# A one-core early-fusion block: the tiles of its expert phase taken in pairs, the down product two pairs behind the gate product

## The chip, the cores and the metric

The kernel runs on one core of one Trainium2 chip. The metric is the device time of one execution in microseconds (us). A core has a matrix engine (PE, with its weight loads, PEld), a vector engine (DVE), an activation engine (ACT), GpSimd (POOL) and a queue engine (SP) that only issues DMAs. Each engine runs its own list of instructions in order; between engines, semaphores are counted up by the one and waited for by the other.

## What is computed

64 images are cut into 36 patches and projected; with a class token and 77 text rows each gives 114 tokens of 256 values, so there are 64 x 114 = 7296 tokens. Then a linear-attention block and a mixture of eight experts follow, each behind a layernorm and with a residual. The change is in the experts:

```python
def _L0_ffn_ref(hidden_states, gate_w, w_gate, w_up, w_down):
    x = hidden_states.reshape(-1, h)
    logits = x @ gate_w.T
    top_v = jnp.max(logits, axis=-1)
    sel = jnp.argmax(logits, axis=-1)
    rw = jax.nn.sigmoid(top_v)
    out = jnp.zeros_like(x)
    for e in range(8):
        mask = (sel == e).astype(x.dtype)
        xs = x * (rw * mask)[:, None]
        g = xs @ w_gate[e].T
        u = xs @ w_up[e].T
        out = out + u * jax.nn.silu(g) @ w_down[e].T
    return out.reshape(b, s, h)
...
h = h + _L0_attn_ref(_layernorm(h, axis=-1), ...)
h = h + _L0_ffn_ref(_layernorm(h, axis=-1), ...)
```

## The kernel before

**Main loop.** 32 pairs of images run through tokeniser, layernorm, attention and routing, to about 345 us. POOL writes every token's row (256 values, and its layernorm's shift and gain and its number) to its place in a list in HBM that is sorted by expert (L652, an indirect DMA for each image, x64). Of 64 tiles of 128 sorted rows, SP loads the first 32 while the loop still runs and the rest once the last image is scattered. The places of the later tiles are worked out in `late_count`, `late_slots` and `late_rows`, which stand in the lists of PE and DVE between the first steps of the expert phase, and so do the routing's last two `tanh` on ACT.

**Expert phase.** Tile t goes through these hands, all in `tile_step(j)`, which each engine runs for j up to 66:

- ACT: xs(t), the layernorm's scale and shift of the rows (L908), four steps ahead.
- PE: turn_x(t), two transposes of xs into PSUM (L1620), two steps ahead; ACT and DVE split them into a high and a low part, xsT_hi (L898) and xsT_lo (L933).
- PE: gate(t), the gate and up products, 2 x 3 matmuls of 256 columns into b_kg (L1351 to L1353).
- ACT: silu of the gate half (L894). DVE: act_u, its product with the up half (L1263).
- PE: turn_a(t), one transpose of act_u (L1629) in step t+1; ACT and DVE split it into actT_hi (L904) and actT_lo (L933).
- PE: down(t), 3 matmuls of 256 columns (L1351 to L1353 into b_w or b_att) in step t+2. DVE: result(t), down plus the row itself, for the residual (L1279), step t+2.
- POOL: an indirect store of result(t) to the output, 131 KB (L716), step t+2.

PE's step j is gate(j), turn_x(j+2), turn_a(j-1), down(j-2). ACT's is silu(j), xsT_hi(j+2), actT_hi(j-1), xs(j+4). DVE's is act_u(j), xsT_lo(j+2), actT_lo(j-1), result(j-2). The order is that of the code, and nothing else chooses it. The expert of a tile is a number in a register of PE, from which the address of its weights is formed before each product (`expert(t)`, L1593; 16 such registers are reloaded in `load_experts`).

Rings: xs and xsT hold four tiles, silu_g, act_u and actT two, result four. turn_x alternates between PSUM banks b_v and b_t, the gate product between the two banks of b_kg. turn_a and down share b_w until tile `SOLO` = 24 and then alternate between b_w and b_att. DVE writes result(t) only when the store of tile t-4 has landed (semaphores stored0 to stored3), and PE writes turn_a and down into a bank only when DVE has read what stood in it.

Of the kernel before, what the change touches and what calls it, by code (L numbers as in the profile page):

```python
# [24 lines left out]
P = 128  # L25
# [46 lines left out]
SOLO = 24  # L72
# [37 lines left out]
def build(nc, x, txt, w_tok, pos, wq, bq, wkgv, wo, wo_rows, bias, bv, bo_col, wgu, wdown, ids, consts, slots, out):  # L110
    scratch = nc.dram_tensor("sorted_rows", (EXPERTS * REGION + P, ROW), F32, kind="Internal").ap()

    with ExitStack() as ctx:
# [83 lines left out]
        with ExitStack() as room:  # L197
# [33 lines left out]
            silu_g = sb("silu_g", [P, 2, INNER], at=room)  # L231
            act_u = sb("act_u", [P, 2, INNER], at=room)
            actT_hi, actT_lo = parts("actT", [P, 2, P], room)
# [25 lines left out]
        def turn_a_bank(t):  # L259

            return (b_w if t.n < SOLO or t.n % 2 == 0 else b_att)[:, 0, 0:P]

        def down_bank(t):

            return (b_w if t.n < SOLO or t.n % 2 == 0 else b_att)[:, 1, 0:D]

# [27 lines left out]
        def b_tile(banks, t, width, start=0):  # L294
            return banks[t.slot(2)][:, start:start + width]
# [102 lines left out]
        DRAIN_B, STEPS_B = 5, range(5, TILES + 3)  # L398
# [185 lines left out]
        def _(pool):  # L584
# [126 lines left out]
            def tile_step(j):  # L711
                if (j - 2).within(TILES):
                    t = j - 2
                    k = t.slot(4)
                    pool.wait_ge(result_ready, t.upto())
                    G.indirect_dma_start(  # L716
                        out=out, out_offset=bass.IndirectOffsetOnAxis(ap=rows_all[:, t.n, ID:ID + 1].bitcast(I32), axis=0),
                        in_=result[:, k, :], in_offset=None,
                        bounds_check=TOKENS - 1, oob_is_err=False).then_inc(stored[k], 16)

            straight(range(0, DRAIN_B), tile_step)
            straight(STEPS_B, tile_step)


        @block.scalar
        def _(act):
# [163 lines left out]
            def tile_step(j):  # L890
                if j.within(TILES):
                    t = j
                    act.wait_ge(gu_done, t.upto())
                    S.activation(silu_g[:, t.slot(2)], b_tile(b_gu, t, INNER), ACT.Silu).then_inc(silu_ready, 1)  # L894
                if (j + 2).within(TILES):
                    t = j + 2
                    act.wait_ge(turn_x_done, t.upto())
                    S.copy(xsT_hi[:, t.slot(4)], b_tile(b_x, t, KC * P).rearrange("p (k t) -> p k t", k=KC)).then_inc(xsT_hi_ready, 1)  # L898
                if (j - 1).within(TILES):
                    t = j - 1  # L900
                    act.wait_ge(turn_a_done, t.upto())
                    if t.had(2):
                        act.wait_ge(down_done, t.upto(2))
                    S.copy(actT_hi[:, t.slot(2)], turn_a_bank(t)).then_inc(actT_hi_ready, 1)  # L904
                if (j + 4).within(TILES):
                    t = j + 4
                    act.wait_ge(row_loaded[t.slot(4)], 16 * t.rounds(4))
                    S.activation(xs[:, t.slot(4)], rows_all[:, t.n, 0:D], ACT.Identity,  # L908
                                 bias=rows_all[:, t.n, SHIFT:SHIFT + 1], scale=rows_all[:, t.n, GAIN:GAIN + 1]).then_inc(xs_ready, 1)
# [14 lines left out]
            straight(STEPS_B, tile_step)  # L924


        @block.vector
        def _(dve):
            V = nc.vector
# [866 lines left out]
```

## Time and profile before

| what | us |
|---|---|
| median of 3 runs (lowest, highest) | 494.29 (491.44, 494.54) |
| the profiled execution | 494.96 |
| its span, first to last instruction | 493.2 |
| mean granted clock of PE, share of full speed | 0.976 |
| main loop, its last work | about 345 |
| expert phase: gate product of tile 0 starts | 359.95 |
| gate product of tile 8 starts | 378.88 |
| gate product of tile 62 starts | 476.37 |
| last instruction ends | 493.17 |

Busy over the whole span: PE 450.4 us (91%), DVE 384.6 (78%), POOL 301.9 (61%), ACT 268.7 (54%). These shares are mostly the main loop's. A row of a timeline gives an instruction's start in us, its length, engine, line, operation, the buffers (out<-in), and in square brackets the idle time of the engine just before it with what ended it; "issue" is time for which the profile shows no wait that ended last. For a group, a number behind x is a count, then come busy time and the mean ns of one. Ends of matmuls are modelled by the profile; their starts are recorded.

### The profile page before, as it was taken

The numbers are of one execution on the slowest core, as the hardware profiler recorded it, in microseconds if no ns is written. First come the engines' busy times: TensorE is split into PE (matmuls) and PEld (weight loads), VectorE is DVE, ScalarE is ACT, GpSimd is POOL, SyncE is SP. The second block draws the span as 40 slices with busy tenths as digits, with TensorE's granted clock in tenths as the row PEclk, the third lists the DMA queues.
The fourth block names the chain that finished last, engine by engine and source line by source line (L and its number), as shares of the span: only waits on it lengthen the run. The fifth ranks groups of instructions, "written<-read, shape, count | busy, mean of one in ns | idle before, by whom it ended". The sixth has DMA issues, their size and how long they took to land. (4 is left out here: it accounts for less than half of the span.)

```text
span 493.2 us, 12451 instructions
## 1 busy us (share of the span) xinstructions
PE 450.4 (91%) x3728; PEld 437.6 (89%) x3728; DVE 384.6 (78%) x1272; ACT 268.7 (54%) x706; POOL 301.9 (61%) x694
## 2 busy tenths in 40 slices
PE   4999999999999999999999999999768989888781
PEld 4999999999999999999999999998757879787770
DVE  5758679999999899989999988977566767676661
ACT  5444455455566566566456356544345667666650
POOL 6405215777777777777777767765565546455453
PEclk9999999999999999999999999999788999999995
DMA  8862122324231321111111211176235762111120
GB/s 290 301 202 83 58 57 69 114 70 119 72 105 32 88 77 33 56 44 35 52 46 35 55 45 44 44 192 165 62 112 161 218 194 76 65 67 62 61 69 13
DMA packets 35007, 46.14 MB, mean 94 GB/s; under 512 B 8937, under 2 KB 27100, under 8 KB 34944
## 3 DMA queue, kind: packets, MB, share of 16 engines
q1 hardware_dynamic: 25722, 30.23, 20.9%
q0 software_dynamic: 9216, 15.12, 10.1%
q8 instruction: 32, 0.52, 0.5%
q14 instruction: 31, 0.25, 0.2%
q10 hardware_dynamic: 6, 0.01, 0.0%
HBM read 26.61 MB, written 17.17 MB: 89 GB/s over the span
## 5 line engine op out<-in xcount | busy, mean ns | idle before, releaser
L716 POOL DMA_INDIRECT out<-result,rows_all x64 | 62.7, 980 | 51.9 <-issue 26.2
L652 POOL DMA_INDIRECT sorted_rows<-rows,place x64 | 78.0, 1218 | 20.3 <-issue 9.7
L800 ACT ACTIVATE den<-b_att,z_eps 114x32 f32<-114x32 f32 x32 | 9.2, 288 | 77.2 <-PE b_att L1465 74.0
L817 ACT ACTIVATE q_exp<-b_w,bq_s 128x228 f32<-128x228 f32 x64 | 28.9, 452 | 29.7 <-PE b_w L1353 29.7
L1263 DVE TENSOR_TENSOR act_u<-b_kg,silu_g 128x128 f32<-128x128 f32 x64 | 18.5, 289 | 30.4 <-ACT silu_g L894 21.2
L1351 PE MATMUL b_kg<-wkgv_hi,xnT_hi 128*114 128x264 f32 x128 | 41.9, 328 | 0.0
L1351 PE MATMUL b_w<-wo_hi,attnT_hi 128*114 128x264 f32 x124 | 41.0, 331 | 0.0
L908 ACT ACTIVATE xs<-rows_all 128x256 f32<-128x256 f32 x64 | 39.4, 617 | 0.0
L1351 PE MATMUL b_kg<-wgu_hi,xsT_hi 128*128 x128 | 37.4, 292 | 1.8 <-issue 1.8
L1351 PE MATMUL b_w<-xnT_hi,wq_hi 128*128 128x256 f32 x128 | 38.6, 301 | 0.4 <-DVE logits L1068 0.3
L894 ACT ACTIVATE silu_g<-b_kg 128x128 f32<-128x128 f32 x64 | 17.8, 278 | 38.7 <-PE b_kg L1353 34.3
L1351 PE MATMUL b_v<-wkgv_hi,xnT_hi 128*114 128x256 f32 x128 | 38.8, 303 | 0.0
L1401 PE MATMUL b_att<-v_sb,k_sb 114*128 114x136 f32 x256 | 37.4, 289 | 0.0
L1465 PE MATMUL b_att<-kv_sb,qT 128*114 128x136 f32 x256 | 35.6, 283 | 1.9 <-DVE qT L1035 1.9
L1353 PE MATMUL b_kg<-wgu_hi,xsT_lo 128*128 x128 | 36.8, 287 | 0.0
L1352 PE MATMUL b_kg<-wgu_lo,xsT_hi 128*128 x128 | 36.6, 286 | 0.0
L1352 PE MATMUL b_kg<-wkgv_lo,xnT_hi 128*114 128x264 f32 x128 | 36.5, 285 | 0.0
L1353 PE MATMUL b_kg<-wkgv_hi,xnT_lo 128*114 128x264 f32 x128 | 36.3, 283 | 0.0
L1352 PE MATMUL b_w<-xnT_lo,wq_hi 128*128 128x256 f32 x128 | 36.1, 282 | 0.0
L1353 PE MATMUL b_w<-xnT_hi,wq_lo 128*128 128x256 f32 x128 | 35.9, 281 | 0.0
L1353 PE MATMUL b_v<-wkgv_hi,xnT_lo 128*114 128x256 f32 x128 | 35.9, 280 | 0.0
L1352 PE MATMUL b_v<-wkgv_lo,xnT_hi 128*114 128x256 f32 x128 | 35.8, 280 | 0.0
(244 smaller groups left out, 1793.8 us busy)
## 6 DMA issues: line engine op xcount, KB each, us to landing
rows_all<-sorted_rows SPq DMA_DIRECT2D x64, 130.0 KB
rows_all<-in_x SPq DMA_DIRECT2D x18, 384.0 KB, 4.7
rows_all<-in_txt SPq DMA_DIRECT2D x32, 154.0 KB
rows_all<-in_wgu SPq DMA_DIRECT2D x8, 256.0 KB, 3.0
rows_all<-patch_out SPq DMA_DIRECT2D x48, 36.0 KB
sorted_rows<-tail_rows SPq DMA_DIRECT2D x9, 130.0 KB
rows_all<-in_wdown SPq DMA_DIRECT2D x8, 128.0 KB, 3.5
sorted_rows<-rows,place POOLq DMA_INDIRECT x64
```

Source lines behind the costliest of these rows:

```text
L652: G.indirect_dma_start(out=scratch[0:EXPERTS * REGION, :], out_offset=bass.IndirectOffsetOnAxis(ap=place[:, k, b:b + 1], axis=0), in_=rows ...
L716: G.indirect_dma_start(out=out, out_offset=bass.IndirectOffsetOnAxis(ap=rows_all[:, t.n, ID:ID + 1].bitcast(I32), axis=0), in_=result[:, k ...
L800: S.activation(den[:].rearrange("p b (k h) -> p b k h", k=KC), heads[:, :, :, P:KVW], ACT.Identity, bias=z_eps[0:TOK, :]).then_inc(den_don ...
L817: S.activation(q_exp[:, c, :], at, ACT.Exp, bias=bq_s[:, c:c + 1])
L894: S.activation(silu_g[:, t.slot(2)], b_tile(b_gu, t, INNER), ACT.Silu).then_inc(silu_ready, 1)
L908: S.activation(xs[:, t.slot(4)], rows_all[:, t.n, 0:D], ACT.Identity, bias=rows_all[:, t.n, SHIFT:SHIFT + 1], scale=rows_all[:, t.n, GAIN: ...
L1263: V.tensor_tensor(act_u[:, t.slot(2)], b_tile(b_gu, t, INNER, INNER), silu_g[:, t.slot(2)], ALU.mult).then_inc(act_ready, 1)
L1351: T.matmul(to, left_hi, right_hi, start=start, stop=False)
L1352: T.matmul(to, left_hi, right_lo, start=False, stop=False)
L1353: return T.matmul(to, left_lo, right_hi, start=False, stop=stop)
L1401: last = T.matmul(b_att[:, b, c * KVW:(c + 1) * KVW], k_sb[:, b, c * P:(c + 1) * P], v_sb[:, b, c, :], start=True, stop=True)
L1465: last = T.matmul(b_att[0:TOK, b, c * KVW:(c + 1) * KVW], qT[:, c, b * TOK:(b + 1) * TOK], kv_sb[:, b, c, :], start=True, stop=True)
```

## The change

Each engine now runs `duo_step(j)` for a pair of tiles (m = tiles 2m and 2m+1), 32 pairs.

- ACT and DVE take both tiles of a pair in one instruction: silu, act_u, xsT_hi, xsT_lo, actT_hi, actT_lo and result, each twice as wide. xs stays an instruction for each tile. For that silu_g, act_u and actT hold four tiles instead of two, and a gate bank, a turn_x bank, a turn_a half and a down half hold both tiles of a pair.
- PE runs the same matmuls for each tile and waits and signals once for a pair. Its step is gate(j), turn_a(j-1), turn_x(j+2), down(j-2), all of pairs. So turn_a now stands before turn_x, and down(j) is two pair-steps behind gate(j).
- DVE's step begins with result(j-3) and then has act_u(j), actT_lo(j-1), xsT_lo(j+2). ACT's is silu(j), actT_hi(j-1), xsT_hi(j+2), then two xs(j+3).
- The result ring still has four tiles, so two pairs: one result instruction waits for both stores of the pair two before it. POOL waits once and then issues both stores.
- The first `tanh`, `late_slots` and `late_rows` stand between pair-steps, where they stood between tile-steps. `SOLO` = 12 pairs is the same tile as before.

The diff's core (the sizes of the rings and what only renames is left out):

```diff
...
-            def tile_step(j):
-                if (j - 2).within(TILES):
-                    t = j - 2
-                    k = t.slot(4)
-                    pool.wait_ge(result_ready, t.upto())
...
+            def duo_step(j):
+                if (j - 3).within(DUOS):
+                    m = j - 3
+                    pool.wait_ge(result_ready, m.upto())
+                    for t in tiles_of(m):
+                        k = t.slot(4)
+                        G.indirect_dma_start(
...
             attention_high(PAIRS - 2)
             S.activation(silu_ahead[:], bq_s[:, 0:1], ACT.Silu)
-            tile_step(Turn(0, -4))
-            tile_step(Turn(0, -3))
+            duo_step(Turn(0, -3))
             tanh(PAIRS - 4)
             denominators(PAIRS - 1)
             tanh(PAIRS - 3)
             attention_high(PAIRS - 1)
-            straight(range(-2, 1), tile_step)
+            straight(range(-2, 1), duo_step)
             tanh(PAIRS - 2)
-            tile_step(Turn(0, 1))
+            duo_step(Turn(0, 1))
             tanh(PAIRS - 1)
-            straight(range(2, DRAIN_B), tile_step)
-            straight(STEPS_B, tile_step)
+            straight(STEPS_B, duo_step)
...
+            def duo_step(j):
+                if (j - 3).within(DUOS):
+                    m = j - 3
+                    dve.wait_ge(down_done, m.upto())
+                    if m.had(2):
+                        for t in tiles_of(m):
+                            dve.wait_ge(stored[t.slot(4)], 16 * t.rounds(4, 4))
+                    V.tensor_tensor(duo(result, m), down_bank(m).rearrange("p (t d) -> p t d", t=DUO),
+                                    rows_all[:, DUO * m.n:DUO * m.n + DUO, 0:D], ALU.add).then_inc(result_ready, 1)
...
-            straight(range(0, 2), tile_step)
+            duo_step(Turn(0, 0))
             late_slots()
-            straight(range(2, 4), tile_step)
+            duo_step(Turn(0, 1))
             late_rows()
-            straight(range(4, 7), tile_step)
-            straight(range(7, TILES + 3), tile_step)
+            straight(STEPS_B, duo_step)
...
+                    pe.wait_ge(xsT_lo_ready, m.upto())
+                    for t in tiles_of(m):
+                        e, to = expert(t), b_gu[m.slot(2)][:, t.slot(2) * D:t.slot(2) * D + 2 * INNER]
+                        for k in range(KC):
+                            last = product(to, (xsT_hi[:, t.slot(4), k, :], xsT_lo[:, t.slot(4), k, :]),
+                                           (wgu_hi[:, bass.ds(e, 1), k, :], wgu_lo[:, bass.ds(e, 1), k, :]), k == 0, k == KC - 1)
                     last.then_inc(gu_done, 1)
...
+                if (j - 1).within(DUOS):
+                    m = j - 1
+                    pe.wait_ge(act_ready, m.upto())
...
+                    for t in tiles_of(m):
+                        last = T.transpose(turn_a_bank(m)[:, t.slot(2) * P:(t.slot(2) + 1) * P], act_u[:, t.slot(4)], ident)
+                    last.then_inc(turn_a_done, 1)
...
+                if (j - 2).within(DUOS):
+                    m = j - 2
+                    pe.wait_ge(actT_lo_ready, m.upto())
...
+                    for t in tiles_of(m):
+                        e = expert(t)
+                        last = product(down_bank(m)[:, t.slot(2) * D:(t.slot(2) + 1) * D], (actT_hi[:, t.slot(4)], actT_lo[:, t.slot(4)]),
+                                       (wdown_hi[:, bass.ds(e, 1), :], wdown_lo[:, bass.ds(e, 1), :]), True, True)
+                    last.then_inc(down_done, 1)
...
```

PE's list in the middle of the expert phase. Before, from turn_x (L1620) over turn_a (L1629) and down into the next gate product; ISA and REGISTER_ALU are the register work on the expert's number:

```order
3177 L1620 MATMUL b_t<-con_s,xs 128x128 [waits xs_ready]
3178 L1620 MATMUL b_t<-con_s,xs 128x128
3179 L1629 MATMUL b_w<-con_s,act_u 128x128 [waits actT_lo_ready,act_ready]
3180 L1351 ISA [waits result_ready,actT_lo_ready]
3181 L1351 MATMUL b_att<-wdown_hi,actT_hi 128x256
3182 L1352 REGISTER_ALU
3183 L1352 MATMUL b_att<-wdown_lo,actT_hi 128x256
3184 L1353 MATMUL b_att<-wdown_hi,actT_lo 128x256
3185 L1351 ISA [waits xsT_lo_ready]
3186 L1351 MATMUL b_kg<-wgu_hi,xsT_hi 128x256
3187 L1352 REGISTER_ALU
3188 L1352 MATMUL b_kg<-wgu_lo,xsT_hi 128x256
```

After, the same place of a pair, from turn_a (now L1630) over turn_x (L1642) and the down products of both tiles:

```order
2741 L1630 MATMUL b_w<-con_s,act_u 128x128 [waits actT_lo_ready,act_ready]
2742 L1630 MATMUL b_w<-con_s,act_u 128x128
2743 L1642 MATMUL b_v<-con_s,xs 128x128 [waits xs_ready]
2744 L1642 MATMUL b_v<-con_s,xs 128x128 x3
2745 L1602 ISA [waits result_ready,actT_lo_ready]
2746 L1360 MATMUL b_w<-wdown_hi,actT_hi 128x256
2747 L1361 REGISTER_ALU
2748 L1361 MATMUL b_w<-wdown_lo,actT_hi 128x256
2749 L1362 MATMUL b_w<-wdown_hi,actT_lo 128x256
2750 L1602 ISA
2751 L1360 MATMUL b_w<-wdown_hi,actT_hi 128x256
2752 L1361 REGISTER_ALU
```

turn_a moved ahead of turn_x and comes in twos; the down product's first tile alone waits; each tile keeps its three matmuls and its register work.

DVE's list there, before, from a result on: L933 is the low part, first of xs, then of the activation:

```order
1148 L1279 TENSOR_TENSOR result<-b_att,rows_all 128x256 [waits stored3,down_done]
1149 L1263 TENSOR_TENSOR act_u<-b_kg,silu_g 128x128 [waits silu_ready]
1150 L933 TENSOR_TENSOR xsT_lo<-b_v,xsT_hi 128x256 [waits xsT_hi_ready]
1151 L933 TENSOR_TENSOR actT_lo<-b_att,actT_hi 128x128 [waits actT_hi_ready]
1152 L1279 TENSOR_TENSOR result<-b_w,rows_all 128x256 [waits stored0,down_done]
1153 L1263 TENSOR_TENSOR act_u<-b_kg,silu_g 128x128 [waits silu_ready]
1154 L933 TENSOR_TENSOR xsT_lo<-b_t,xsT_hi 128x256 [waits xsT_hi_ready]
1155 L933 TENSOR_TENSOR actT_lo<-b_w,actT_hi 128x128 [waits actT_hi_ready]
1156 L1279 TENSOR_TENSOR result<-b_att,rows_all 128x256 [waits stored1,down_done]
```

After, a whole pair-step and the next result (L1275, was L1279):

```order
1104 L1275 TENSOR_TENSOR result<-b_w,rows_all 128x512 [waits stored1,stored0,down_done]
1105 L1280 TENSOR_TENSOR act_u<-b_kg,silu_g 128x256 [waits silu_ready]
1106 L942 TENSOR_TENSOR actT_lo<-b_w,actT_hi 128x256 [waits actT_hi_ready]
1107 L942 TENSOR_TENSOR xsT_lo<-b_t,xsT_hi 128x512 [waits xsT_hi_ready]
1108 L1275 TENSOR_TENSOR result<-b_att,rows_all 128x512 [waits stored3,stored2,down_done]
```

Eight instructions for two tiles became four, result moved to the head of the step, actT_lo moved ahead of xsT_lo, and a result waits for two stores.

ACT's list at the first tiles, before, from silu of tile 0: L765 is the routing's `tanh`:

```order
457 L894 ACTIVATE silu_g<-b_kg 128x128 [waits gu_done]
458 L898 CAST xsT_hi<-b_v 128x256 [waits turn_x_done]
459 L908 ACTIVATE xs<-rows_all 128x256 [waits row_loaded0]
460 L765 ACTIVATE tanh_top<-top_n 114x2 [waits field_step,top_n_ready]
461 L894 ACTIVATE silu_g<-b_kg 128x128 [waits gu_done]
462 L898 CAST xsT_hi<-b_t 128x256 [waits turn_x_done]
463 L904 CAST actT_hi<-b_w 128x128 [waits turn_a_done]
464 L908 ACTIVATE xs<-rows_all 128x256 [waits row_loaded1]
465 L765 ACTIVATE tanh_top<-top_n 114x2 [waits field_step,top_n_ready]
```

After, from silu of pair 0:

```order
459 L902 ACTIVATE silu_g<-b_kg 128x256 [waits gu_done]
460 L913 CAST xsT_hi<-b_v 128x512 [waits turn_x_done]
461 L918 ACTIVATE xs<-rows_all 128x256 [waits row_loaded2]
462 L918 ACTIVATE xs<-rows_all 128x256 [waits row_loaded3]
463 L773 ACTIVATE tanh_top<-top_n 114x2 [waits field_step,top_n_ready]
464 L902 ACTIVATE silu_g<-b_kg 128x256 [waits gu_done]
465 L909 CAST actT_hi<-b_w 128x256 [waits turn_a_done]
466 L913 CAST xsT_hi<-b_t 128x512 [waits turn_x_done]
467 L918 ACTIVATE xs<-rows_all 128x256 [waits row_loaded0]
468 L918 ACTIVATE xs<-rows_all 128x256 [waits row_loaded1]
469 L773 ACTIVATE tanh_top<-top_n 114x2 [waits field_step,top_n_ready]
```

Each `tanh_top` stands behind the work of a pair instead of a tile, and actT_hi moved ahead of xsT_hi.

## Rows read from the trace of the kernel before

**Rows 1.** Windows: length; PE, PEld, DVE, ACT, POOL busy (count); PEclk, DMA share, GB/s.

```profile
359.95:378.88 18.93, 14.91 (x94) 13.73 (x95) 11.56 (x44) 9.38 (x32) 13.22 (x30) 0.82 0.44 132
378.88:476.37 97.49, 84.81 (x650) 76.81 (x649) 66.63 (x217) 65.59 (x216) 52.61 (x54) 1.00 0.34 107
476.37:493.17 16.80, 4.60 (x29) 3.40 (x27) 4.02 (x13) 1.45 (x7) 6.13 (x7) 0.70 0.10 33
```

**Rows 2.** Timeline, PE, one unstalled tile step: start, length, line, operation.

```profile
430.55 0.38 PE L1620 MATMUL b_v<-con_s,xs 128*128 128x128 f32 x2
430.76 0.27 PE L1629 MATMUL b_att<-con_s,act_u 128*128 128x128 f32 x1
...
431.22 0.28 PE L1351 MATMUL b_kg<-wgu_hi,xsT_hi 128*128 x1
...
431.93 0.38 PE L1620 MATMUL b_t<-con_s,xs 128*128 128x128 f32 x2
```

**Rows 3.** Groups by shape, ACT: out<-in, shapes, count, busy us, mean ns.

```profile
L894 ACT ACTIVATE silu_g<-b_kg 128x128 f32<-128x128 f32 x64 | 17.8, 278 | 38.7 <-PE b_kg L1353 34.3 <-issue 3.8 <-remote 0.4
L898 ACT CAST xsT_hi<-b_v 128x256 fp32r<-128x256 f32 x32 | 12.0, 375 | 2.2 <-PE b_v L1620 1.4 <-PE b_t L1620 0.4
...
L791 ACT COPY v_sb<-b_v 114x512 f32<-114x512 f32 x18 | 10.6, 587 | 11.7 <-PE b_v L1353 10.8 <-issue 0.9
```

**Rows 4.** Groups by shape, DVE, columns as above.

```profile
L1060 DVE TENSOR_TENSOR rows<-b_w,rows_all 114x512 f32<-114x512 f32 x31 | 21.4, 692 | 9.5 <-PE b_w L1353 7.8 <-issue 1.7
...
L1263 DVE TENSOR_TENSOR act_u<-b_kg,silu_g 128x128 f32<-128x128 f32 x64 | 18.5, 289 | 30.4 <-ACT silu_g L894 21.2 <-issue 9.0
L1279 DVE TENSOR_TENSOR result<-b_w,rows_all 128x256 f32<-128x256 f32 x44 | 18.4, 419 | 3.2 <-PE b_w L1353 1.4 <-remote 1.3
```

**Rows 5.** Timeline, all engines, around a late signal (tile 48).

```profile
450.60 0.98 POOL L716 DMA_INDIRECT out<-result,rows_all  x1 [0.30 <-issue]
450.66 0.28 PE L1353 MATMUL b_kg<-wgu_hi,xsT_lo 128*128 x1
...
452.07 0.98 POOL L716 DMA_INDIRECT out<-result,rows_all  x1 [0.49 <-issue]
...
452.18 0.38 PE L1620 MATMUL b_t<-con_s,xs 128*128 128x128 f32 x2
...
453.00 0.28 ACT L894 ACTIVATE silu_g<-b_kg 128x128 f32<-128x128 f32 x1 [2.15 <-PE b_kg L1353]
...
453.66 0.33 PE L1629 MATMUL b_w<-con_s,act_u 128*128 128x128 f32 x1 [1.10 <-issue]
...
454.24 0.41 DVE L1279 TENSOR_TENSOR result<-b_w,rows_all 128x256 f32<-128x256 f32 x1
...
455.45 0.98 POOL L716 DMA_INDIRECT out<-result,rows_all  x1 [2.41 <-DVE result L1279]
```

**Rows 6.** Waits, 378 to 478 us: waiter, releaser, total us, times, longest.

```profile
ACT silu_g L894 <- PE b_kg L1353: 25.1, 33, 2.2
```

**Rows 7.** Timeline, POOL and DVE: stores of tiles 58 and 59, result of 63.

```profile
476.92 0.98 POOL L716 DMA_INDIRECT out<-result,rows_all  x1 [0.30 <-issue]
...
478.41 0.98 POOL L716 DMA_INDIRECT out<-result,rows_all  x1 [0.51 <-issue]
...
482.59 0.42 DVE L1279 TENSOR_TENSOR result<-b_att,rows_all 128x256 f32<-128x256 f32 x1 [0.39 <-PE b_att L1353]
```

**Rows 8.** Busy time by stretch after the store at 476.92; DMA share, GB/s last.

```profile
478.25:479.00 0.75, 0.36 (x4) 0.16 (x2) 0.00 (x0) 0.00 (x0) 0.59 (x1) 1.00 0.50 175
```

**Rows 9.** Timeline, ACT, PE and POOL where the first tiles meet the last pair.

```profile
362.62 0.19 ACT L765 ACTIVATE tanh_top<-top_n 114x2 f32<-114x2 f32 x1
...
367.60 0.20 ACT L765 ACTIVATE tanh_top<-top_n 114x2 f32<-114x2 f32 x1 [3.01 <-POOL top_n L627]
...
369.04 0.30 PE L1629 MATMUL b_w<-con_s,act_u 128*128 128x128 f32 x1 [2.57 <-DVE actT_lo L933]
...
371.81 1.01 POOL L716 DMA_INDIRECT out<-result,rows_all  x1 [0.30 <-issue]
```

More of the change, by code:

```diff
@@ L230, in build @@
             xsT_hi, xsT_lo = parts("xsT", [P, 4, KC, P], room)
-            silu_g = sb("silu_g", [P, 2, INNER], at=room)
-            act_u = sb("act_u", [P, 2, INNER], at=room)
-            actT_hi, actT_lo = parts("actT", [P, 2, P], room)
+            silu_g = sb("silu_g", [P, 4, INNER], at=room)
+            act_u = sb("act_u", [P, 4, INNER], at=room)
+            actT_hi, actT_lo = parts("actT", [P, 4, P], room)
             result = sb("result", [P, 4, D], at=room)
@@ L292, in build, with duo, tiles_of @@
         tile_ends = b_att[0:1, 1, EARLY_AT + 32:EARLY_AT + 32 + ENDS_W]
-        def b_tile(banks, t, width, start=0):
-            return banks[t.slot(2)][:, start:start + width]
+        def duo(ring, m):
+            first = m.slot(2) * DUO
+            return ring[:, first:first + DUO]
+        def tiles_of(m):
+            return [Turn(0, DUO * m.n + k) for k in range(DUO)]
         s_const = sem("s_const")
@@ L888, in _ @@
                 step(i)
[L890 to L909, printed above, removed]
@@ new lines, in duo_step @@
+            def duo_step(j):
+                if (j - 3).within(DUOS):
+                    m = j - 3
+                    dve.wait_ge(down_done, m.upto())
+                    if m.had(2):
+                        for t in tiles_of(m):
+                            dve.wait_ge(stored[t.slot(4)], 16 * t.rounds(4, 4))
+                    V.tensor_tensor(duo(result, m), down_bank(m).rearrange("p (t d) -> p t d", t=DUO),
+                                    rows_all[:, DUO * m.n:DUO * m.n + DUO, 0:D], ALU.add).then_inc(result_ready, 1)
+                if j.within(DUOS):
+                    m = j
+                    dve.wait_ge(silu_ready, m.upto())
+                    V.tensor_tensor(duo(act_u, m), b_gu[m.slot(2)].rearrange("p (t w) -> p t w", t=DUO)[:, :, INNER:], duo(silu_g, m),
+                                    ALU.mult).then_inc(act_ready, 1)
+                if (j - 1).within(DUOS):
+                    m = j - 1
+                    dve.wait_ge(actT_hi_ready, m.upto())
+                    low(duo(actT_lo, m), turn_a_bank(m).rearrange("p (t n) -> p t n", t=DUO), duo(actT_hi, m)).then_inc(actT_lo_ready, 1)
+                if (j + 2).within(DUOS):
+                    m = j + 2
+                    dve.wait_ge(xsT_hi_ready, m.upto())
+                    low(duo(xsT_lo, m).rearrange("p t k n -> p (t k n)"), b_x[m.slot(2)],
+                        duo(xsT_hi, m).rearrange("p t k n -> p (t k n)")).then_inc(xsT_lo_ready, 1)
@@ new lines, in duo_step @@
+                if (j + 2).within(DUOS):
+                    m = j + 2
+                    if m.n == 0:
+                        pe.wait_ge(v_ready, PAIRS)
+                    if m.n == 1:
+                        pe.wait_ge(attnT_lo_ready, PAIRS - 1)
+                    pe.wait_ge(xs_ready, m.upto())
+                    for t in tiles_of(m):
+                        for k in range(KC):
+                            at = (t.slot(2) * KC + k) * P
+                            last = T.transpose(b_x[m.slot(2)][:, at:at + P], xs[:, t.slot(4), k * P:(k + 1) * P], ident)
+                    last.then_inc(turn_x_done, 1)
```

125 lines of the change are left out of this document (50 added, 75 removed).

## The prediction

> **What bounds the kernel now.** I read the page's slices first: PE is full up to about 345 us and the change leaves those instructions alone. Then I cut the expert phase into stretches by the starts of its gate products [rows 1]. The middle one, tiles 8 to 62, is 54 tiles in 97.49 us, 1.81 us a tile, at a granted clock of 1.00. No engine is full in it: PE 84.81, DVE 66.63, ACT 65.59, POOL 52.61. So the phase is bound by waiting between engines, and the question is what is waited for.
>
> The timeline of PE gives the step without a stall [rows 2]: from one turn_x (430.55) to the next (431.93) is 1.38 us, of it turn_x 0.21, turn_a and down 0.46, gate 0.71. 54 x 1.38 = 74.5, so 97.49 - 74.5 = 23.0 us are lost in this stretch, 0.43 a tile. The others have room in a 1.38 step: DVE 66.63 / 54 = 1.23, ACT 1.21. Their instructions are short, 0.28 to 0.42 us, and wider ones cost little more [rows 3, 4].
>
> The timeline around tile 48 shows how the loss arises [rows 5]. PE's last matmul of gate(48) starts at 450.66 and ends, by the model, at 450.94. silu, which waits for it alone, starts at 453.00, 2.06 us later. silu and act_u follow at once, and turn_a starts at 453.66, 0.66 after silu's start. PE had finished its turn_x at 452.56 and stood for 1.10. So gate's signal came late, not ACT. In this order PE has turn_x 0.21, turn_a and down 0.46, the next gate 0.71 and turn_x 0.21 between the end of gate(t) and turn_a(t), 1.59 us. The chain needs 0.66, so a signal may be late by 0.93 for nothing, and 2.06 - 0.93 = 1.13 is the stall seen. The waits view says how often: ACT's silu waited 25.1 us for PE in 33 waits, the longest 2.2 [rows 6]. What makes the signal late the trace doesn't say. Two facts stand near it: silu started (453.00) just as the second of two POOL stores ended (452.07 + 0.98 = 453.05), and PE's register work on the expert's number exists in this phase.
>
> A rule bears on this. In the Trainium skill, "Perfetto Trace Analysis", section "Tensor Engine Instruction (MATMUL, LD_WEIGHTS)", a matmul's reported end is an estimate, and its semaphore goes out only when PSUM has acknowledged the writes. By that rule the 2.06 need not be a delay between engines: PE itself may be behind its records, which is the third rival below.
>
> **The change part by part, per pair of tiles.**
>
> PE: the same matmuls and register instructions, so 2 x 1.38 = 2.76 us without a stall. Fewer waits are worth nothing where the step has no stall.
>
> ACT: silu two of 0.278 become one of 0.375, -0.18; actT_hi likewise -0.18; xsT_hi two of 0.375 become one of 0.587 (the nearest row of that width) -0.16 [rows 3]. 2 x 1.21 = 2.43 becomes 1.91. DVE: act_u two of 0.289 become 0.419, -0.16; actT_lo the same; xsT_lo and result two of 0.419 become 0.692, -0.15 each [rows 4]. 2.47 becomes 1.85. Both hide under PE's 2.76 before and after; the direct gain is nothing. POOL: two stores of 0.98 with 0.30 between, 2 x 1.28 = 2.56 [rows 5], still under 2.76, but its cover is only 0.20.
>
> The order is what counts. After, between the end of gate(j) and turn_a(j) PE has turn_a(j-1), turn_x(j+2), down(j-2) and gate(j+1), the whole 2.76. The chain grows by the wider silu and act_u, 0.66 + 0.10 + 0.13 = 0.89. So the room is 1.87 where it was 0.93. The stall of tile 48 would shrink from 1.13 to 0.19, and there is one gate signal for two tiles. Queued behind turn_a on PE stand turn_x(j+2) and down(j-2); down(j-2) has a step more than it needs.
>
> Bounds of the step: nothing lost, 1.38 a tile; all the loss stays, 1.81. By tile 48 alone nearly everything is won; against that, turn_x, turn_a and down send signals too, whose lateness I can't read, and a pair's results arrive at DVE and POOL in lumps. I take the middle, 1.60. Gain in the middle stretch: 54 x (1.81 - 1.60) = 11.3 us.
>
> The result ring. It holds two pairs, so result(m) waits for both stores of m-2. The loop is result 0.69 [rows 4], result's end to the store's start 0.80 (454.65 to 455.45 [rows 5]), stores 0.98 + 0.30 + 0.98, and landing L: 3.75 + L against two steps, 5.52 at 1.38 a tile, 6.40 at 1.60. L from below: the store that ended at 476.92 + 0.98 = 477.90 [rows 7] still moved data at 175 GB/s from 478.25 to 479.00 [rows 8], 0.75 x 175 = 131 KB, its whole size, so L is at least 1.10. From above: result(63), which needs the store of tile 59 (478.41 + 0.98 = 479.39), stood at 482.59 [rows 7], so L is at most 3.20. The loop is 4.85 to 6.95. Since the data ended at 1.10, I take L near 1.1 to 1.6, and the ring costs nothing.
>
> The Trainium skill, "DMA: Bandwidth & Descriptors", section "Anatomy of one DMA — SWDGE (gpsimd) path", gives such a DMA about 2.0 us fixed, most of it the write's receipt, beside its bytes. An estimate with that behind the second issue, 3.75 + 2.0 + 0.30 = 6.05, is 1.51 us a tile: by it the relief would stop at about 478 us, and by the rows it needn't. No row here times the receipt.
>
> Start. The last two tanh were issued at 362.62 and 367.60, the second after 3.01 of waiting for POOL; PE stood 2.57 before 369.04, and the first store left at 371.81 [rows 9]. After, the second tanh stands behind a pair's work more, so it and what POOL does after it come later by a tile or two (1.4 to 2.8 us); but when it is done, PE and ACT are about two tiles further. Net 0, bounds -3 and +3. Drain: the last pair passes turn_a, down, result and two stores; fewer instructions, wider ones, one step more. -0.3, bounds -0.5 and +0.7.
>
> Sum: 494.96 (the profiled execution: span 493.2 and 1.8 around it) - 11.3 + 0 - 0.3 = 483.4. The median of the runs is 0.7 below the profiled one, so 483.
>
> **The rivals.** (1) Near-full relief: T = 1.38 to 1.50, 494.96 - 54 x 0.43 - 0.3 = 471 to 494.96 - 16.7 - 0.3 = 478. For it: tile 48's own arithmetic. Against: other signals, and POOL's 2.56 of 2.76 leaves no slack for a lump. (2) The ring binds: L near its upper bound, 6.95 / 4 = 1.74 a tile, 494.96 - 3.8 - 0.3 = 491; with L at 2.9, 1.66 and 487. For it: result(63) came so late. Against: 131 KB had moved by 1.10. (3) The change doesn't do what it says: the late signals are PE's own pace with these instructions, a register operation and three or six matmuls a tile, all unchanged. Then T stays 1.78 to 1.85 and the time 493 to 497. For it: the profile's ends are modelled and PE issues the same list; against: PE's unstalled steps of 1.38 hold the same register work. (4) Slower: the stores now leave in streaks. If a store holds back signals (453.00 against 453.05 [rows 5]), a streak holds one for 0.98 + 0.30 + 0.98 and the 0.61 from the store's end (453.05) to turn_a (453.66), 2.87; less the room of 1.87 that is 1.0 a pair, T = 1.88, 494.96 + 3.8 - 0.3 = 498.5, and with the start's bound up to 502. It decides where a pair's gate signal is later than 1.87 + 0.86 = 2.73 us on the mean (0.86 is what two tiles lose now). Against: the longest wait seen is 2.2 [rows 6], although stores already followed each other at 0.30 and 0.49 there.
>
> **How the numbers follow.** Partial relief (1.50 to 1.68, 478 to 488) 0.42; near-full relief 0.18; the ring 0.10; unchanged pace 0.20; slower 0.10. A measurement of this kernel tells about 1% from nothing: 489.4 and 499.2 are the marks. Faster: 0.42 + 0.18 + 0.07 of the ring's = 0.67. Same: 0.20 + 0.03 = 0.23. Slower: 0.10. The range 472 to 495 leaves out the slower case, about 0.05 of the unchanged pace above 495 and 0.02 below 472, 0.17 in all.
>
> **What would show it.** In the changed kernel's windows, gate to gate over the pairs 4 to 31 (54 tiles) should take about 86 us (1.60 a tile), with PE's 84.8 busy nearly filling it; 75 means full relief, 96 or more none. PE's waits for act_u before turn_a should be few and short; silu's waits for PE may stay late. DVE's result should not be released by a store; if it is, the ring binds. silu should be one instruction near 0.375, act_u near 0.42. The second tanh should start near 369 to 370. Wrong it would be above all if PE's step of a pair never comes near 2.76: then the loss was PE's own.

## The result, and the profile after

The kernel after took 495.68 us (median of 20 runs, 493.02 to 499.18) beside 493.78 for the kernel before (20 runs): a ratio of 1.0036, interval 1.0019 to 1.0054. The forecast was 483. The change moved the time by less than 1%, and upwards. The profiled execution took 496.18 us, its span 494.4, at a mean granted clock of 0.966.

The stretches of the kernel after by its gate products: start to pair 4 (tile 8), pair 4 to pair 31 (tile 62), and the rest. Columns as in [rows 1].

```profile
358.60:371.79 13.19, 12.20 (x87) 11.23 (x88) 9.37 (x33) 7.68 (x20) 9.25 (x25) 0.88 0.34 105
371.79:471.87 100.08, 84.93 (x646) 80.28 (x645) 55.79 (x107) 57.71 (x132) 53.24 (x55) 0.93 0.36 110
471.87:494.40 22.53, 6.17 (x36) 5.15 (x34) 4.39 (x9) 1.13 (x3) 9.82 (x11) 0.71 0.14 45
```

The middle takes 100.08 us where it took 97.49, 1.85 a tile. Its gate products come 7.1 us earlier at pair 4 and 4.5 earlier at pair 31, because gate products now run further ahead of the results. So the results compare better: that of pair 4 starts at 386.85 and that of pair 31 at 483.63, 96.8 us, where tiles 9 and 63 stood at 386.71 and 482.59, 95.9 us. The rate of finished tiles is what it was, 1.79 us against 1.78.

DVE and ACT did get lighter: DVE is busy 55.79 us instead of 66.63, ACT 57.71 instead of 65.59. The groups by shape between 378 and 478 us, columns as in [rows 3]:

```profile
L1280 DVE TENSOR_TENSOR act_u<-b_kg,silu_g 128x256 f32<-128x256 f32 x27 | 11.4, 424 | 24.8 <-ACT silu_g L902 15.8 <-issue 8.8
L902 ACT ACTIVATE silu_g<-b_kg 128x256 f32<-128x256 f32 x27 | 10.4, 383 | 30.4 <-PE b_kg L1362 23.8 <-remote 5.9 <-issue 0.5
```

PE is at a granted clock of 0.93 in the middle, where it was at 1.00. In slices of 20 us (the last of 17) the clock column, third from the right, reads 0.86, 0.97, 0.91, 1.00 and 0.90:

```profile
378.00:398.00 20.00, 16.01 (x107) 14.55 (x107) 10.49 (x21) 11.04 (x26) 8.83 (x9) 0.86 0.77 222
...
418.00:438.00 20.00, 16.98 (x130) 16.28 (x129) 11.14 (x23) 12.11 (x29) 10.53 (x11) 0.91 0.20 69
```

Missing clock is 2.8 + 0.6 + 1.8 + 0 + 1.7 = 6.9 us of full speed. It is counted over PE's waits too, so that is the most it can have cost; the kernel before reads 1.00 in all five slices. The parts at the lower level (1.2 GHz) come behind waits of PE: from 427 to 433 us, around its wait of 2.10 at 428.29 (below), the granted clock is 0.76.

Where PE stood, the waits view of PE says, 372 to 484 us (waiter, releaser, total us, times, longest):

```profile
PE b_t L1642 <- ACT xs L918: 7.4, 6, 2.0
PE b_att L1630 <- DVE act_u L1280: 2.1, 1, 2.1
PE b_att L1630 <- issue: 1.9, 1, 1.9
PE b_w L1630 <- issue: 1.8, 2, 1.2
PE b_v L1642 <- ACT xs L918: 1.6, 2, 0.8
```

turn_x waiting for ACT's xs is new; the kernel before has no such wait in its middle. Within the middle stretch alone PE waited 4.5 us before turn_a (L1630) and 9.6 before turn_x (L1642), whatever ended the wait.

The timeline around the latest signal shows the mechanism (PE's rows between left out but for the last matmuls of a gate product):

```profile
422.62 0.69 DVE L1275 TENSOR_TENSOR result<-b_w,rows_all 128x512 f32<-128x512 f32 x1 [0.32 <-DMA out<-result,rows_all]
422.66 0.98 POOL L725 DMA_INDIRECT out<-result,rows_all  x1 [0.30 <-issue]
...
422.79 0.28 PE L1362 MATMUL b_kg<-wgu_hi,xsT_lo 128*128 x1
...
424.10 0.98 POOL L725 DMA_INDIRECT out<-result,rows_all  x1 [0.46 <-issue]
...
425.39 0.98 POOL L725 DMA_INDIRECT out<-result,rows_all  x1 [0.30 <-issue]
...
425.92 0.28 PE L1362 MATMUL b_kg<-wgu_hi,xsT_lo 128*128 x1
427.39 0.38 ACT L902 ACTIVATE silu_g<-b_kg 128x256 f32<-128x256 f32 x1 [4.83 <-PE b_kg L1362]
...
428.29 0.44 PE L1630 MATMUL b_att<-con_s,act_u 128*128 128x128 f32 x2 [2.10 <-DVE act_u L1280]
```

The gate product ends at 423.07 and its silu starts at 427.39, 4.32 us late, 1.02 after the last of a row of POOL stores ended (426.37). Meanwhile PE went through turn_a, turn_x, down and a whole further gate product. In the trace's semaphore records PE's signals for this gate, turn_a, turn_x, down and the next gate stand at 427.37, 427.41, 427.47, 427.55 and 427.67, and the one before them at 422.30. PE did 3 us of work after the gate whose signals then came out within 0.30 us. So they were held back, not late because PE was slow. Only PE's were: of the signals from 372 to 482 us that can be matched to their instruction, 50 of PE's 102 stand over 0.1 us behind its end, while those of ACT (80) and DVE (86) all stand 0.01 behind. Some records are missing for each engine.

### The profile page after: what moved, and what is told of

Same layout as the page of the kernel before. It is cut to its first block, busy times and chain, and to the rows that moved or that the text cites. A ratio compares the mean times of both kernels' runs of the same rounds, so it can differ in the third digit from the quotient of the medians.

```text
span 494.4 us, 11973 instructions
## 1 busy us (share of the span) xinstructions
PE 449.1 (91%) x3728; PEld 440.0 (89%) x3728; DVE 373.0 (75%) x1144; ACT 260.1 (53%) x610; POOL 300.9 (61%) x694
## 4 chain that ended last, share of the span: by engine, by line
PE 82%; ACT 4%; issue 4%; DVE 3%; another core or an unknown queue 2%; POOL 2%; DMA 1%; POOLq 0%; SPq 0%; DVEq 0%
PE b_w L1360 7%; PE b_kg L1362 7%; PE b_w L1361 7%; PE b_w L1362 7%; PE b_kg L1360 7%; PE b_att L1410 7%; PE b_kg L1361 6%; PE b_att L1474 6%; PE b_v L1360 3%; PE b_v L1362 3%; PE b_v L1361 3%; PE b_t L1488 2%; PE b_t L1423 2%; ACT xs L918 2%
## 5 line engine op out<-in xcount | busy, mean ns | idle before, releaser
L1360 PE MATMUL b_kg<-wgu_hi,xsT_hi 128*128 x128 | 38.4, 300 | 0.2
L1361 PE MATMUL b_kg<-wgu_lo,xsT_hi 128*128 x128 | 37.6, 293 | 0.0
L1280 DVE TENSOR_TENSOR act_u<-b_kg,silu_g 128x256 f32<-128x256 f32 x32 | 13.6, 424 | 29.4 <-ACT silu_g L902 18.5
L1361 PE MATMUL b_w<-wo_lo,attnT_hi 128*114 128x264 f32 x124 | 35.7, 288 | 0.0
L1362 PE MATMUL b_w<-wo_hi,attnT_lo 128*114 128x264 f32 x124 | 35.6, 287 | 0.0
```

Of the source, the lines that this page charges most:

```text
L1280: V.tensor_tensor(duo(act_u, m), b_gu[m.slot(2)].rearrange("p (t w) -> p t w", t=DUO)[:, :, INNER:], duo(silu_g, m), ALU.mult).then_inc(ac ...
L1360: T.matmul(to, left_hi, right_hi, start=start, stop=False)
L1361: T.matmul(to, left_hi, right_lo, start=False, stop=False)
L1362: return T.matmul(to, left_lo, right_hi, start=False, stop=stop)
```

## The experiments

**What the chips do.** The groups of runs met two kinds of conditions. In one the kernel before takes 493 to 495 us (the comparison above and the runs c, d and g; "late chips" below), in the other 475.0 to 475.6 (e and f; "prompt chips"). The record numbers the chips 15 (c), 1 (d) and 14 (g), and 1 (e) and 3 (f). The number 1 stands on both sides, 26 minutes apart, and the record doesn't say whether it is the same chip. So "late" and "prompt" name what a group met, and not a property of the chip that was shown. Within one group the kernel before was timed between the others and stayed on its side. The main loop takes the same time on both (in the kernel after the first silu starts at 360.7 to 361.6 on late chips and at 362.6 on a prompt one). Each run stands beside the kernel before of its own group, and a theory's letter holds within its group. I measure lateness as silu's start minus the modelled end of its gate product, mean over all silu (good to about 0.02 us). It also counts time in which ACT was still busy. The signal records tell the two apart: in d3, d4 and all e and f runs every gate signal stands 0.01 us behind its gate's end, so what lateness these have (0.08 to 0.15) is ACT's own queue in the first pairs.

**e1 and e2: no register work.** In the kernels after and before:

```diff
-                return pe.snap(expert_of[...][...], min_val=0, max_val=EXPERTS - 1)
+                return t.n // 8
```

> The kernel after, but the expert of tile t is the constant t//8 instead of a number read from a table into PE registers: the same matmuls, no register work on PE (the output is that of other experts, since each tile meets fixed weights). In the kernel after the results of pairs 4 to 31 span 386.85 to 483.63, 96.8 us for 54 tiles, 1.79 a tile, as before. Theory A (PE's late signals come from the register work): with it gone the same stretch falls to 75 to 82 us and the time to about 475 to 482. Theory B (the streaks of POOL stores hold PE's signals back): no change, 94 to 98 us and 494 to 497. Theory C (the ring of two pairs of results binds): no change either.

> The kernel before with the same edit: constant experts, no register work on PE (the output is that of other experts). Theory A: the 0.43 us a tile lost goes, about 75 to 80 us for 54 tiles and a time of 473 to 478. Theory B: unchanged, 492 to 495.

**e3 and e4: other stores, a larger ring**, in the kernel after:

```diff
+                    act.wait_ge(result_ready, m.upto())
+                    for t in tiles_of(m):
+                        act.dma_start(out[t.n * TOK:(t.n + 1) * TOK, :], result[0:TOK, t.slot(4), :]).then_inc(stored[t.slot(4)], 16)
```

```diff
-            result = sb("result", [P, 4, D], at=room)
+            result = sb("result", [P, 6, D], at=room)
...
-                    if m.had(2):
+                    if m.had(3):
```

> The kernel after, but the results are stored by plain DMAs that ACT issues, 114 of each tile's 128 rows to consecutive rows of the output (the rows land in the wrong places), and POOL issues no store. Theory B: PE's signals are no longer late, silu follows the gate product, the stretch of results falls to 75 to 82 us and the time to 475 to 482. Theory A: still 94 to 98 us. Theory C: a plain store lands sooner, so this falls too, but PE's signals are late as before.

> The kernel after with room for six results (three pairs) instead of four; nothing else differs. Theory C: DVE's waits for a landed store (3.0 us in 404 to 475 and 3.5 at the last pair) go, and with them several us, to 488 or less. Theories A and B: at most 1 to 3 us, since those waits are 6.5 us in all and stand beside late signals.

Measured beside 475.0 for the kernel before: e1 472.3 (ratio 0.9938, 0.9907 to 0.9968), e2 471.9 (0.9914), e3 484.1 (1.0195), e4 468.7 (0.9877, 0.9854 to 0.9899). The stretch of results was 77.4, 75.2, 89.3 and 74.7 us. All expectations had been written for a chip of 494 us, and the first reading of e1 and e2, that the register work was the cause, would have been wrong: this chip had no late signals in any of the four (lateness 0.12 to 0.14). What they do show: without the register work both orders take 0.6 to 0.9% less than the kernel before, e3 was held up by its own landings (DVE waited 31.1 us for them), and e4 runs at 1.38 us a tile.

**c1 to c4: the same on a late chip**, with both kernels as controls.

> The kernel before, unchanged, for a profile beside those of the same chip: on the chip of e1 to e4 it took 475.0 us, where it took 493.8 on the chip of the main comparison, and no profile of it from there exists. Theory A (PE signals come late because of what one chip does, and how late differs from chip to chip): on a chip where it takes about 475, the results of tiles 9 to 63 span about 78 to 80 us (1.44 to 1.48 a tile) instead of 95.9, silu waits little over 1 us at the longest for the gate product; on a chip where it takes about 494, the rows repeat those of before: 95 to 97 us, waits of 2.0 to 2.3. Theory B (the 19 us lie elsewhere, in the main loop or the start): the stretch is 95 us on either.

> The kernel after, unchanged. Theory A on a chip of 475 us: signals come on time, PE could go at 1.38 a tile, and the ring of two pairs is what is left: results of pairs 4 to 31 span 77 to 80 us with DVE waiting over 20 us for landed stores, the time 471 to 476, so no gain over before there either. On a chip of 494 us: 95 to 98 us, 494 to 497.

> The kernel after with constant experts (tile t takes expert t//8, so the output is that of other experts; no register work on PE), the edit of e1 again, now beside the kernel after itself. Theory R (register work delays PE's signals): faster than c2 by 10 us or more on a chip of 494 us, where the delay is large; by under 3 us on a chip of 475. Theory S (the delay has another source): within 3 us of c2 on either.

> The kernel after with six result tiles (e4 again, beside the kernel after itself). On a chip of 475 us: 3 to 6 us below c2, as the ring is what binds there (theory C). On a chip of 494 us: theory C says 5 us or more below c2 as well; if late signals bind, within 3 us of c2.

Before 492.99: c1 493.35, c2 495.13 (1.0020, 0.9985 to 1.0055), c3 488.57 (0.9921, 0.9890 to 0.9951), c4 493.58 (1.0022). Lateness 0.60 (before), 1.16, 1.00 and 1.09. Without the register work the kernel is 6.6 us faster than c2 by the medians (4.9 by the ratios), under the 10 of theory R and over the 3 of S; its signals are nearly as late (1.00 against 1.16, the longest 4.93). So the register work costs something here, which these runs don't explain, but isn't what holds signals. The larger ring gives 1.6 us by the medians and nothing by the ratios: it isn't the bound on such a chip.

**d1 to d4: POOL's stores taken away on a late chip.** d3 is the kernel after with ACT's plain stores and six result tiles, d4 the kernel before with ACT's plain stores.

> The kernel before, unchanged, for its profile on whichever chip this is. On a chip of about 494 us: the rows of before, silu's lateness behind the gate product 0.6 us on the mean. On a chip of about 475: under 0.2 us on the mean, results of tiles 9 to 63 in 75 to 80 us.

> The kernel after, unchanged. On a chip of about 494 us: 494 to 497, silu 1.1 us late on the mean. On a chip of about 475: signals on time and the ring of two pairs left as the bound, results of pairs 4 to 31 in 77 to 80 us with over 20 us of DVE waiting for landed stores, and a time of 471 to 475, within 1% of before.

> The kernel after with plain stores issued by ACT instead of POOL's indirect ones (114 rows of each tile to consecutive rows, so they land in the wrong places), and six result tiles so that slower landings don't bind. Theory S1 (POOL's store activity holds back PE's signals on chips of 494 us): silu's mean lateness falls from 1.1 to under 0.2 us there, and the stretch of results from 97 to under 82 us. Theory S2 (the lateness is PE's own on such a chip): lateness stays near 1 us and the stretch over 92 us. On a chip of 475 us both say: lateness 0.14, and 75 to 85 us.

> The kernel before with the same plain stores issued by ACT, one per tile (four result tiles). S1: on a chip of 494 us mean lateness falls from 0.6 to under 0.2 us; S2: it stays near 0.6. The time itself also carries slower landings of these stores (e3 had DVE waiting 31 us for them), so the lateness is what is read.

Before 494.28: d1 496.03, d2 500.43 (1.0095, 1.0058 to 1.0132), d3 466.99 (0.9418, 0.9358 to 0.9479), d4 470.03 (0.9510). Lateness 0.61, 1.28, 0.15 and 0.13; stretch of results 94.2, 100.6, 78.9 and 79.3 us. d2 came out above its 494 to 497. Without POOL's stores the late signals are gone in both orders, as S1 says, and the time is 24 to 27 us below the kernel before. Not all of that need be the signals: late and prompt groups differ by 17 to 20 us for the unchanged kernel before.

**f1 to f4 and g1, g2: the stores alone, half of them, and spaced.** f1 (and g1) adds to d3

```diff
+                    pool.wait_ge(result_ready, m.upto())
+                    for t in tiles_of(m):
+                        G.indirect_dma_start(
+                            out=aside, out_offset=bass.IndirectOffsetOnAxis(ap=rows_all[:, t.n, ID:ID + 1].bitcast(I32), axis=0),
+                            in_=rows_all[:, t.n, 0:D], in_offset=None,
+                            bounds_check=TOKENS - 1, oob_is_err=False).then_inc(put_aside, 16)
```

f2 (and g2) lets POOL store only `tiles_of(m)[0]` and ACT the other tile; f3 puts behind each store of the kernel after

```diff
+                        G.memset(spare[:], 0.0).then_inc(spared, 1)
```

> The kernel of d3 (ACT stores the results by plain DMAs in the wrong places, six result tiles), and beside it POOL issues the kernel after's 64 indirect stores again, but of the input rows into a buffer that nobody reads; nobody waits for them before the end. Theory S1 (POOL's store activity holds PE's signals back): on a chip of about 494 us silu's mean lateness goes from 0.15 (d3) to about 1 us and the stretch of results from 79 to over 90 us, the time from 467 to 478 or more. Theory S3 (it is the landing of the results, or the wait of POOL for them, that matters): stays at 0.15 and 79 us, 467 to 469. On a chip of about 475 us: no lateness either way.

> Six result tiles; of each pair the first tile is stored by POOL's indirect store as in the kernel after, the second by a plain DMA of ACT into a buffer aside (so half the output is not written). POOL is in a store 0.98 of some 3 us. If the lateness comes of streaks (one store after another without a gap): under 0.2 us on the mean and 77 to 82 us for the stretch, a time of 465 to 470. If every store holds signals back for its own time: about half of the kernel after's lateness, 0.4 to 0.6 us, 85 to 90 us for the stretch.

> The kernel after with a small memset of POOL (256 columns of a spare buffer, some 0.3 us) behind each store, so that no two stores follow each other at 0.30 us. If streaks are the cause: the lateness falls below 0.5 us, POOL's own rate (about 2 x 1.65 = 3.3 us a pair) becomes the bound, the stretch 88 to 92 us and the time 486 to 491 on a chip of about 494 us. If every store counts alike: no gain, 494 to 500.

> The kernel after, unchanged, as control. On a chip where before takes about 475 us: signals on time, DVE waits over 20 us for landed stores, results of pairs 4 to 31 in 76 to 80 us, 471 to 475 in all. On a chip of about 494 us: silu 1.1 to 1.3 us late on the mean, 97 to 101 us, 494 to 501.

> The kernel of f1 again: plain stores of ACT carry the results (to wrong places), and POOL issues 64 indirect stores of input rows into a buffer aside. Where before takes about 475 us it took 488.9 with silu's mean lateness 0.10, held up by landings (DVE waited 30.7 us for them). Theory S1 (POOL's store activity holds PE's signals back) on a chip of about 494 us: mean lateness 0.8 us or more, and the time clearly above 489. Theory S3 (it is the results' own stores): lateness stays at 0.1 to 0.2, 488 to 490.

> The kernel of f2 again (of each pair the first tile stored by POOL, the second by ACT into a buffer aside; half the output is not written). Where before takes about 475 us it took 463.7 with lateness 0.13. On a chip of about 494 us: if only streaks of stores hold signals back, 0.1 to 0.2 us of lateness and 463 to 467; if every store does for its own time, 0.4 to 0.6 us and 470 or more.

The f runs met a prompt chip, before 475.62: f1 488.92, f2 463.68, f3 480.21, f4 475.21 (0.9989, 0.9967 to 1.0011), lateness 0.10 to 0.15 in all. So f3 says nothing about streaks where signals are late; its 1.0102 goes with POOL's slower rate (0.98 + 0.33 + 0.17 = 1.48 us a store) and with 26.5 us in which DVE waited for landed stores. That was not repeated on a late chip. f2 came out a little below its 465 to 470, and f4 had 16.0 us of waits for landed stores where over 20 were expected.

g met a late chip, before 495.23: g1 499.77, g2 463.62 (0.9376). In g1 the results travel as in d3 and nobody waits for POOL, and yet lateness is 1.19 instead of 0.15. The longest one, with POOL's stores in a row before it:

```profile
435.69 0.28 PE L1371 MATMUL b_kg<-wgu_hi,xsT_lo 128*128 x1
...
436.22 0.98 POOL L729 DMA_INDIRECT aside<-rows_all  x1 [0.30 <-DVE result L1284]
...
437.50 0.98 POOL L729 DMA_INDIRECT aside<-rows_all  x1 [0.30 <-issue]
...
438.79 0.98 POOL L729 DMA_INDIRECT aside<-rows_all  x1 [0.31 <-issue]
441.05 0.38 ACT L906 ACTIVATE silu_g<-b_kg 128x256 f32<-128x256 f32 x1 [5.58 <-remote]
```

Silu's gate product ended at 435.97; it started 5.08 us later, 1.28 after the sixth store of the row ended (it began at 432.37). Adding POOL's stores brings the late signals back. In g2 each store stands alone, as POOL's timeline shows:

```profile
423.12 0.98 POOL L728 DMA_INDIRECT out<-result,rows_all  x1 [1.79 <-DVE result L1283]
425.89 0.98 POOL L728 DMA_INDIRECT out<-result,rows_all  x1 [1.79 <-DVE result L1283]
```

Lateness is 0.21, against the 0.4 to 0.6 expected if every store counted alike, and the pair takes 425.89 - 423.12 = 2.77 us. Even the 0.21 is not theirs: from pair 6 on every gate signal of g2 stands 0.01 us behind its gate's end. Single stores at this spacing hold nothing; what holds signals is rows of stores with hardly a gap. That it is the row and not the number of stores is read from traces, since g2 also has half the stores. In the kernel before POOL is in stores for 0.53 of the time both from 380 to 415 us, in rows of one and two and while rows are still loaded, where no silu is over 0.7 us late, and from 418 to 475, mostly in rows of three and four. There, rows of four end at 427.5, 453.05, 466.01 and 479.39, and the silu of tiles 34, 48, 55 and 62 start at 427.49, 453.00, 465.98 and 479.34, the first 1.05 and the others 2.06 to 2.10 late; after rows of three (ends at 420.7, 434.1, 439.4, 446.3, 459.2, 472.6) silu is 1.2 to 1.4 late. From tile 8 on no other silu is over 1 us late, but for the one right behind a late one, which finds ACT busy. After the change all rows are of four and six: the first silu a row of four holds is 0.9 to 2.2 us late, that of a row of six 1.9 to 4.3.

What a prompt chip makes of the kernel after, f4: DVE's results in its steady state,

```profile
426.06 0.68 DVE L1275 TENSOR_TENSOR result<-b_w,rows_all 128x512 f32<-128x512 f32 x1
...
428.83 0.68 DVE L1275 TENSOR_TENSOR result<-b_att,rows_all 128x512 f32<-128x512 f32 x1
...
431.60 0.68 DVE L1275 TENSOR_TENSOR result<-b_w,rows_all 128x512 f32<-128x512 f32 x1
```

a pair every 2.77 us, 1.38 a tile, nothing lost. But before 404 us, while rows are loaded, the ring binds (waits of f4, 378 to 404 us):

```profile
DVE result L1275 <- DMA out<-result,rows_all: 7.5, 8, 1.6
```

Over 378 to 478 us that wait is 16.0 us in f4 (the other 8.5 from 446 us on, behind one slow landing) and 3.4 us with six result tiles (e4).

## Why the prediction was wrong, point by point

**The bound and the unstalled step: right.** 1.38 us a tile is what PE does when nothing is late (2.77 a pair in f4, g2). Widths: silu 0.375 foretold, 0.383 measured; act_u 0.419, 0.424. DVE and ACT were busy 2.07 and 2.14 us a pair, more than the 1.85 and 1.91 foretold, and still under PE's 2.77; their relief was worth nothing.

**"I take the middle, 1.60": the term that failed.** It was 1.79 by results, 1.85 by gate products. Two things are wrong in the step that led to it: what the room would have to hold, and the room itself.

First, the lateness was taken over unchanged from the kernel before (2.06 at tile 48, 2.2 at the longest [rows 5, 6]), and only the room for it was made larger, from 0.93 to 1.87. But the lateness is made by POOL's stores (d3, g1), in rows as far as g2 and the traces tell, and the change makes these rows longer: each pair hands POOL two stores at once, and a held pair becomes four or six in a row. [rows 5] shows two stores before tile 48's silu, and I took them for the row; they are the last of four:

```profile
448.03 0.98 POOL L716 DMA_INDIRECT out<-result,rows_all  x1 [1.74 <-DVE result L1279]
449.31 0.98 POOL L716 DMA_INDIRECT out<-result,rows_all  x1 [0.30 <-issue]
```

The lateness grew to 4.32 and 3.41 at the longest (1.50 of the 3.41 is ACT still busy behind a held pair), its mean from 0.60 to between 1.10 and 1.28, for half as many silu. The room doubled and so did what had to fit in. This is the fourth rival, whose mechanism I had: it priced the hold at 2.87 for a row of two and gave 1.88 a tile and 498.5 us. That price was wrong too: before the change a row of two holds 0.6 to 0.7, and the mean stayed far under the 2.73 that the rival needed. That its 1.88 lies near the 1.85 is luck.

Second, the room of 1.87 is turn_a's alone. What else is queued behind silu in ACT's list I didn't price. Before, xs(j+4) was needed by PE two steps later; after, xs(j+3) stands behind silu, actT_hi and xsT_hi and is needed in the next step. The rows of one pair that just fits (silu's start to the end of both xs, and the turn_x that needs them):

```profile
418.12 0.38 ACT L902 ACTIVATE silu_g<-b_kg 128x256 f32<-128x256 f32 x1 [0.71 <-PE b_kg L1362]
...
419.14 1.11 ACT L918 ACTIVATE xs<-rows_all 128x256 f32<-128x256 f32 x2
...
420.30 0.65 PE L1642 MATMUL b_v<-con_s,xs 128*128 128x128 f32 x4
```

From silu to the end of xs is 2.13 us. An unstalled PE comes to that turn_x a step (2.77) after the one that begins 0.05 after the gate product (423.12 against 423.07), so 2.82 after its end: the room on this way is about 0.7. PE's waits for xs are 9.0 us, more than its four largest other waits together (6.9). The longest, where the gate signal came 3.0 late and both xs ended at 461.32:

```profile
461.37 0.90 PE L1642 MATMUL b_t<-con_s,xs 128*128 128x128 f32 x3 [1.97 <-ACT xs L918]
```

These waits repeat in the controls, 9.3 us in c2 and 13.5 in d2, and there are none in f4. So the second fault weighs more than the first. The 1.60 left 54 x 0.22 = 11.9 us for losses; the waits before turn_a, 4.5, and the clock, at most 6.9, would have fitted into that, and the 9.6 before turn_x did not (an estimate from the waits above). Both kinds of wait begin with a held signal, so less of either would be left if none were held. No run gave xs more depth, so this part is read from the trace and not tested.

**The clock** was not in the sum at all: up to 6.9 us at the lower level, where before had none. In f4 the kernel after kept 1.00 from 378 us until PE ran out of tiles.

**The ring.** On late chips right, it costs little (c4 against c2, at most 1.6 us), though five results of the kernel after were released by a store (6.6 us of waits), which the prediction named as a sign against it. As a general statement wrong: "I take L near 1.1 to 1.6". The results that a store released in f4 started 1.55 to 1.57 us after the store's end once rows were loaded (one, at 446.83, 3.17), and 2.4 to 3.2 while they still were. With 3.75 + 3.0 = 6.75 against 5.54 for two steps the ring binds there, and the second rival is what eats most of the gain on a prompt chip: with six result tiles the kernel is 1.2% faster than before (e4), with four it isn't (f4, 0.9989); these are runs of two groups.

The rule of the Trainium skill that I weighed ("DMA: Bandwidth & Descriptors", "Anatomy of one DMA — SWDGE (gpsimd) path", about 2.0 us fixed) gave 1.51 a tile; f4's quiet stretch has 0.98 + 1.56 = 2.54 from a store's start to the wait's end, near the page's 2.0 + 0.3, and 1.38 a tile. The page's figure runs from the issue, and I had set it behind the issue.

**Start and drain.** Foretold net 0 and it was 0.1 (386.85 against 386.71). The second tanh started at 368.17, not at 369 to 370, after 1.94 of waiting instead of 3.01. The drain was to gain 0.3: PE's last down did end early, but the last result waited 3.54 us for a landed store and started 1.0 later than before:

```profile
483.63 0.69 DVE L1275 TENSOR_TENSOR result<-b_att,rows_all 128x512 f32<-128x512 f32 x1 [3.54 <-DMA out<-result,rows_all]
```

**The third rival** (PE's own pace) named the time that came, 493 to 497, and its reason is refuted: d3 has the same matmuls and register work and takes 467. Its doubt about the modelled ends was of use, and the semaphore records settle it: held signals come in a bunch, and in d3 all 113 recorded signals of PE from 372 to 482 us stand 0.01 us behind the modelled end, so the model is right where nothing holds them.

**What stays open.** Why PE's signals are held during rows of POOL stores in some groups of runs and not in others; on prompt chips f1 has rows of up to fourteen (gaps to 0.52 us) with lateness 0.10. Whether it is the chip or something in its surroundings can't be told from these runs; that chip number 1 stands on both sides leaves the second at least possible. Whether spacing all 64 stores helps on a late chip was not tried there, nor whether a plain store issued by POOL holds signals as its indirect ones do. A kernel with the right output that is faster on both kinds wasn't found: e4's is faster on prompt chips (468.7 against 475.0) and equal on late ones (c4, 1.0022).

## What to carry to other kernels

A late signal is a quantity with a cause, and a change that makes room for it must be asked whether it also feeds the cause: here work in twos gave POOL's stores in rows of four and six, and rows of them hold PE's signals. When an instruction waits longer, look at everything behind it in its queue and at the step in which each is needed, not only at the chain it belongs to. A ring's loop has to be reckoned with the landing time of the busiest stretch, and a kernel and its control should be timed together, and in more than one group of runs, before a mechanism is believed.

## What the runs showed of the hardware that I had not expected

In some groups of runs PE's semaphore signals, and not those of ACT or DVE, are held back, up to 5.1 us (g1), while POOL issues indirect stores one after another at gaps of 0.3 to 0.5 us; PE itself goes on working, and the held signals then come within 0.3 us, some 0.6 to 1.3 us after the row of stores ends, or about at its end. The same kernel costs 493 to 495 us in these groups and 475 in the others. Single stores with 1.79 us between (g2) do nothing of the sort: with half the stores left to POOL the kernel takes 463.6 and 463.7 us on the two kinds.
